# Perceiver block on one Trainium2 core: where the row-maximum matmuls stand among scores and projections in the cross-attention

## The reference, cut to what matters

```python
q = (query @ Wq + bq)            # 128 x 256, 16 heads of 16
k = (key_value @ Wk + bk)        # 12544 x 256
v = (key_value @ Wv + bv)
attn = softmax(clip(einsum(q, k) * D**-0.5, -1e4, 1e4))
x = einsum(attn, v) @ Wo + bo
```

## Time and profile before

| | |
|---|---|
| runs, median (lowest to highest) | 1286.22 us (1282.94 to 1286.94) |
| the profiled execution, its own time | 1283.76 us |
| its span | 1281.9 us |
| mean granted TensorE clock | 0.959 of 2.4 GHz |
| PE busy (matmuls) | 1140.6 us, 89% of the span |
| VectorE busy | 726.4 us, 57% |
| ScalarE busy | 711.3 us, 55% |
| GpSimd busy | 202.3 us, 16% |
| maxima, matmuls (line 542 through 653) | 896, 312.6 us, mean 369 ns |
| maxima, reductions (line 1260) | 896, 536.0 us, mean 621 ns |
| exponentials (line 995) | 784, 404.6 us, mean 601 ns |

### The profile page before, as it was taken

One profiled execution on the slowest core, in us unless ns is written; L12 is line 12 of the kernel. 1 busy time (PEld: TensorE's weight loads), 2 busy tenths in 40 slices (PEclk: granted clock), 3 DMA queues, 4 the chain that ended last, 5 costly groups with the idle time before them and its releaser, 6 DMA issues.

```text
span 1281.9 us, 30526 instructions
## 1 busy us (share of the span) xinstructions
PE 1140.6 (89%) x13043; PEld 744.5 (58%) x13043; DVE 726.4 (57%) x1356; ACT 711.3 (55%) x1387; POOL 202.3 (16%) x114
## 2 busy tenths in 40 slices
PE   7899999999999999717799999999999999999777
PEld 4355566565556565517696355655565556665565
DVE  2566566665566664488323556665666666665343
ACT  3356666666666657352212356666666666667422
POOL 0222222222121110000000222222121222220000
PEclk9799999999999999857999799999999999999889
DMA  9544444443344350440905735443344444360360
GB/s 211 137 116 116 116 116 105 99 114 100 99 104 116 84 175 3 151 146 1 321 8 117 186 85 125 111 106 100 97 112 116 110 109 103 80 166 3 131 222 5
DMA packets 83929, 144.92 MB, mean 113 GB/s; under 512 B 9993, under 2 KB 73361, under 8 KB 83281
## 3 DMA queue, kind: packets, MB, share of 16 engines
q1 hardware_dynamic: 82896, 142.85, 42.1%
q10 hardware_dynamic: 896, 0.12, 0.1%
HBM read 64.64 MB, written 0.15 MB: 51 GB/s over the span
## 4 chain that ended last, share of the span: by engine, by line
PE 68%; ACT 13%; DVE 13%; issue 3%; DMA 2%; SPq 0%; ACTq 0%; DVEq 0%
PE ring L542 37%; PE st L542 15%; PE ot L542 14%; ACT work L995 6%; DVE mpart L1260 5%; ACT arena L960 2%; ACT arena L978 2%; DVE arena L1399 1%; PE ring L692 1%; ACT work L1001 1%; DMA arena<-rows 1%; DMA wkv<-L_wkv 1%; SPq L386 0%; DMA qst<-rowb 0%; DMA warena<-ctxT 0%
## 5 line engine op out<-in xcount | busy, mean ns | idle before, releaser
L1260 DVE TENSOR_REDUCE mpart<-ring 128x1 f32<-128x448 f32 x896 | 536.0, 621 | 352.5 <-PE ring L542 344.7
L995 ACT ACTIVATE work<-st 128x512 f32<-128x512 f32 x784 | 404.6, 601 | 156.2 <-PE st L542 156.0
L542 PE MATMUL ring<-arena,qst 96*128 96x448 bf16 x896 | 312.6, 369 | 44.8 <-ACT arena L960 20.7
L542 PE MATMUL ot<-work,arena 128*17 128x128 f32 x6272 | 233.7, 276 | 8.9 <-ACT work L995 1.9
L542 PE MATMUL st<-qst,arena 97*128 97x128 bf16 x3136 | 237.6, 219 | 1.5 <-DMA qst<-rowb 1.5
L542 PEld LDWEIGHTS st<-qst,arena 97*128 97x128 bf16 x3136 | 206.2, 98 | 42.4 <-issue 7.5
L503 POOL TENSOR_TENSOR arena<-arena 128x896 f32<-128x896 f32 x52 | 98.1, 1887 | 644.1 <-ACT arena L967 643.8
L542 PEld LDWEIGHTS ot<-work,arena 128*17 128x17 f32 x6272 | 142.0, 97 | 85.3 <-ACT work L995 51.2
L542 PEld LDWEIGHTS ring<-arena,qst 96*128 96x128 bf16 x896 | 83.2, 97 | 183.9 <-issue 81.9
L542 PE MATMUL ring<-wkv,warena 64*128 64x256 f32 (+1 forms) x784 | 155.7, 395 | 3.9 <-ACT arena L978 3.2
L542 PE MATMUL ring<-warena,wkv 128*128 128x448 f32 x448 | 151.8, 578 | 2.7 <-DMA warena<-ctxT 1.3
(11 more groups left out here) (281 smaller groups left out, 651.5 us busy)
## 6 DMA issues: line engine op xcount, KB each, us to landing
arena<-arena SPq DMA_DIRECT2D x336, 224.0 KB, 3.6
arena<-ffn_W SPq DMA_DIRECT2D x16, 1024.0 KB, 13.1
warena<-ctxT SPq DMA_DIRECT2D x28, 448.0 KB, 3.8
warena<-ctxT SPq DMA_DIRECT2D x56, 224.0 KB, 4.5
arena<-f SPq DMA_DIRECT2D x2, 4096.0 KB, 25.1
arena<-scratch_bc SPq DMA_DIRECT2D x1, 2048.0 KB, 7.1
arena<-rows SPq DMA_DIRECT2D x1, 1792.0 KB, 6.9
warena<-w_in_proj SPq DMA_DIRECT2D x1, 1024.0 KB
```

What stands on the lines that cost most here:

```text
L542: return nc.tensor.matmul(o, l, r, start=start, stop=stop, **kw)
L995: nc.scalar.activation(pbuf[:, n % 2, half * 512:(half + 1) * 512], st[:, 2 * (n % 2) + half], ACT.Exp).then_inc(*signal(f"{lay}_exp_done"))
L1260: V.reduce_max(mpart[:, 2 * h + hf:2 * h + hf + 1], ring[:, BANKS[step][0], 0:HALF], AX_X).then_inc(*signal(f"{lay}_b_max"))
```

## The change

In each double unit, the maxima are dealt out otherwise. Before, a quarter of them (rounded down) stood ahead of each of the two score units and a quarter behind the second, then came the projections, then the rest. Now the first score unit stands right behind the two `pv`, one maximum stands between the two score units, all others but one stand behind the second, ahead of the projections, and one stands behind the projections. In a double unit without projections (`made` is 0) none is left over, and all but the first stand behind the second score unit.

```diff
             limit = c + 1 if w < 4 else c + 2
             n = per_pair[w]
-            plan += some(n // 4, limit) + score(c * UNITS + 2 * w + 2) + some(n // 4, limit)
-            plan += score(c * UNITS + 2 * w + 3) + some(n // 4, limit)
+            made = (w in values and c + 2 < NCH) or (w in keys and c + 3 < NCH)
+            plan += score(c * UNITS + 2 * w + 2) + some(1, limit) + score(c * UNITS + 2 * w + 3)
+            plan += some(n - 1 - made, limit)
             if w in values and c + 2 < NCH:
                 plan += [("v", c + 2, k) for k in values[w]]
             if w in keys and c + 3 < NCH:
                 plan += [("k", c + 3, k) for k in keys[w]]
-            plan += some(n - 3 * (n // 4), limit)
+            plan += some(made, limit)
```

## The result

The changed kernel takes 1313.47 us in the median (1312.68 to 1317.74, four runs) against 1285.43 us (1282.94 to 1286.94, four runs) for the kernel before: a ratio of 1.0231, 95% interval 1.0212 to 1.025, 28 us slower. 1318.5 was forecast, 1304 to 1330 the range. The profiled execution has a span of 1311.7 us against 1281.9, and a granted clock of 0.961 against 0.959.

The account below looks back on a forecast made before the run. TensorE's queue order (68% of the chain) bounds the kernel. Ten steady chunks +12.0, chunk 0 +2.4, chunks 11 and 12 +2.5: 16.9 per attention, 33.8 for both, on 1283.8 gives 1317.6; given as 1318.5, range 1304 to 1330.

Parts of the forecast that it names:

- The replaced wait: At ring steps behind bunched maxima: waits for ScalarE give way to VectorE's, a bank freed 1.07 us after its maximum starts.
- The first rival: At the projections: ScalarE waits go, no new one comes, bank b1 free within 0.62 us; -46 us, 1240; chance 0.05.
- The sum by double unit: Steady chunk, new less old: units 0 to 4 -0.01, +0.46, -0.07, -0.08, +0.46; unit 5 +0.57, then -0.13; total +1.20 us.
- The 0.10 of a longer pair: At projection pairs: after an idle TensorE a pair takes 0.10 us longer, 2.62 against 2.52.
- The mis-sized term: From double unit 5's pair to the next chunk's first `pv`: ScalarE's line hides TensorE's earlier arrival; -0.13 us, from the `ot` copy.
- The step to the median: Whole kernel: profiled execution forecast at 1317.6, the runs' median 2.5 us above the profiled one, 1318.5 given.
- the second rival: Units 1, 4, 5: extra 1.49 us swallowed by exponentials starting 0.2 earlier; a wash, 1284 to 1290; chance 0.05.
- The ends: Chunks 11 and 12: five units without a pair at +0.45 at most, less about 0.15, and the rest; +2.5 us.
- The wash: Same as the second rival: new waits equal old ones in four units, exponentials swallow the extra; chance 0.05.
- The third rival: Whole kernel: TensorE loses a further 2% of clock in longer gaps, +18 us, 1336; chance 0.08.
- The rule on rotating banks: At PSUM banks: rotating independent groups overlaps evacuation with the next matmuls; read so, the change gains, giving the first rival's time.

Follow-up runs that it names:

- half the reduction: Changed kernel with each row maximum over 224 of 448 columns and queries scaled down by 16: 1271.23 us; same edits in the kernel before: 1272.40 us.
- the first experiment: Changed kernel, one maximum still behind the projections, the others dealt out as before the change: 1258.57 us, ratio 0.9789 to the kernel before.
- the broken-up order: Changed kernel, one maximum behind the projections, a quarter between the two `pv`, a quarter between the score units, the rest behind the second: 1271.27 us, ratio 0.9897.

## Why the prediction was right

- **The replaced wait.** Right, to 0.01 us: the bank is free 1.07 to 1.08 behind the maximum's start (215.02 to 216.10, 221.48 to 222.55), and 0.84 with half the reduction. The first rival had it free within 0.62; the waits for VectorE and the 42 us of the halved reduction rule it out.
- **The sum by double unit.** In the chunk shown above and what follows it in the trace, forecast and measured: unit 0 from the end of `pv` 5.46 and 5.45 (213.93 to 219.38), unit 1 3.77 and 3.76, unit 2 6.02 and 6.01, unit 3 6.12 and 6.12, unit 4 3.38 and 3.38, unit 5 up to the pair's end 5.83 and 5.83 (238.65 to 244.48). VectorE's addition for `o`, for which I charged nothing, cost nothing here: the first reduction behind it starts the usual 0.40 behind its matmul (224.59 to 224.99). The 0.10 of a longer pair was right in size, but the account, a TensorE that had run idle, was not: the first experiment shows it at a pause of 0.04.
- **The mis-sized term** is the one behind double unit 5. I gave -0.13 for ScalarE's line, from the assumption that its instructions start at each other's end. It is -0.29: the pair ends at 208.98 and `pv` at 213.93, 4.95 us, against 5.24 before (202.23 to 207.47). The ends of the two pairs, first before and then after:

```profile
202.23 0.36 PE L542 MATMUL ring<-arena,qst 96*128 96x448 bf16 x1
```
```profile
208.98 0.36 PE L543 MATMUL ring<-arena,qst 96*128 96x448 bf16 x1
```

ScalarE's timeline in the changed kernel there:

```profile
209.10 1.16 ACT L961 ACTIVATE arena<-ring,cols_sb 128x448 f32<-128x448 f32 x2 [2.08 <-PE ring L543]
210.15 0.94 ACT L972 CAST arena<-arena 128x896 bf16<-128x896 f32 x1
210.97 0.60 ACT L1002 COPY work<-ot 128x512 f32<-128x512 f32 x1
211.45 2.08 ACT L996 ACTIVATE work<-st 128x512 f32<-128x512 f32 x4
```

The copy starts 0.82 behind a cast that lasts 0.94, and the exponentials 0.48 behind a copy of 0.60. I had used the distance, not the duration, for VectorE's reductions (0.53 against 0.62), and not for these. The Trainium skill, Perfetto Trace Analysis, section Optimizing Scalar/DVE Operations, says that the write-acknowledgement part of a profiled duration overlaps with the next instruction; both engines' rows agree. 0.16 over 20 chunks is 3.2 of the 5.8 us between the forecast difference (33.8) and the timed one (28.0). Another 1.8 is no error of the sum: the two profiled executions differ by 29.9 us, the medians by 28.0.
- **The step to the median.** The working ends at 1317.6 and adds 2.5 us for the median, which is 1320.1 and not the 1318.5 that it gives; likewise the second rival's own figures give 1292, not 1284 to 1290. The range, 1304 to 1330, holds 1320.1 as well.
- **The ends.** Forecast 2.5 us for chunks 11 and 12 in each attention. The second has 2.37 (from its 11th `o` step to its last, 60.80 before and 63.17 after). The first has 0.46 (63.46 and 63.92), where the kernel before is the odd one: its granted clock was 0.97 over that stretch against 1.00 in its second attention, and 1.00 in both of the changed kernel. It also waited 1.46 us for the row's transfer there, against 1.21 after. With chunk 0 and what follows up to the first `o` (+2.61 and +2.78 against about 2.7), the pieces add up to 2.61 + 10.36 + 0.46 + 2.78 + 10.67 + 2.37 = 29.3, of the 29.8 between the spans.
- **The wash.** The exponentials do start earlier, but `pv` could give back only 0.12 and 0.22, as its rows had said.
- **The clock.** The third rival did not come: the granted clock is 1.00 in the steady stretch (95 to 135 us), and in all there are 188 waits for VectorE at gaps up to 0.3 in the records. The row that the rival rested on (0.93 at 465 to 490 us) is no case of such waits: the one long gap there is the 1.46 us for the row's transfer, and the changed kernel has 1.21 at that place and a clock of 1.00. What the Trainium skill says of micro-idles (TensorE: Matmul & The Clock Gate, section A second HAM failure mode: psum-queue depth-cycling) did not show at gaps of this size.
- **The rule on rotating banks** of the Trainium skill (Perfetto Trace Analysis, section Matmuls), which spoke for a gain, holds in the first experiment and not in the changed kernel, with the same three banks. In these runs rotation hides a maximum's reduction only where 1.07 us of work stands between its start and the third ring step behind it.

## What to carry to other kernels

When buffers are dealt round-robin to several kinds of steps, a move changes the wait of every step that follows in the ring, also of kinds that the move does not touch. For each step, take the distance in the producer's queue to the step whose buffer it inherits, and compare it with that buffer's whole turnaround (start of the producer, start and length of the consumer, release). A fix for one late consumer, here ScalarE, should be made alone: one maximum of each pair moved from behind the projections to ahead of them gave 26 us, and bunching the rest with it cost 55.

## What the runs showed of the hardware

- To put a bfloat16 maximum between two float32 `pv` groups costs TensorE 0.23 us of its queue beyond the maximum's own 0.20, although nothing waits.
- A pair of projections whose first weight load has to wait for the bank takes 0.10 us longer from its start to the next matmul's (2.99 and 2.66 against 2.89 and 2.55), whether TensorE stood still for nearly 0.5 us ahead of it (216.10 in the changed kernel) or for 0.04 (206.47 in the first experiment).
- The weight load of a score unit behind a maximum starts 0.19 us ahead of its matmul; at a change between a maximum and `pv` it starts with it (220.36 in the broken-up order). Why is not shown.
